# A fused kernel's first stage: one-row indices, counts by column, and a new order of loads and DVE work

## The reference

```python
# x (128, 64, 512), conditions (128,), weights (200, 64, 64), W1 (2048, 512), W2 (512, 2048)
w = weights[conditions]
c = jnp.einsum('bct,bcd->bdt', x, w)           # rows of 512

def ternarize(W, threshold=0.05):
    absW = jnp.abs(W)
    delta = threshold * jnp.max(absW)
    mask = absW > delta
    n = jnp.maximum(jnp.sum(mask), 1)
    alpha = jnp.sum(jnp.where(mask, absW, 0.0)) / n
    return alpha * jnp.sign(W) * mask

h = gelu(c @ ternarize(W1).T + b1)             # exact gelu
y = h @ ternarize(W2).T + b2
scale = jnp.max(jnp.abs(y)) / 7 + 1e-8
out = x + jnp.clip(jnp.round(y / scale), -7, 7) * scale
```

## Time and profile before

| | us |
|---|---|
| median of 3 runs (1003.8 to 1004.51) | 1003.95 |
| the profiled execution, its own time | 1004.09 |
| its span in the profile | 1002.2 |
| PE busy | 925.8 (92%) |
| DVE busy | 644.5 (64%) |
| ACT busy | 547.3 (55%) |
| POOL busy | 144.8 (14%) |

### The profile page before, as it was taken

The page is one execution under the profiler, slowest core; times in us unless marked ns, Lnnn a source line. Parts: engine busy times, 40 slices in busy tenths (PEclk is TensorE's granted clock), DMA queues, the critical chain, the costliest instruction groups (busy, mean ns, idle before and its releaser), DMA issues.

```text
span 1002.2 us, 14662 instructions
## 1 busy us (share of the span) xinstructions
PE 925.8 (92%) x5136; PEld 440.1 (44%) x5136; DVE 644.5 (64%) x1024; ACT 547.3 (55%) x690; POOL 144.8 (14%) x187
## 2 busy tenths in 40 slices
PE   2999999999999999999999999999999999999700
PEld 2544444444444444444444444444444444444300
DVE  7998576665656666656657666665666665633493
ACT  6886728274473827365372827446382836536190
POOL 4400030301203030200203030110303030000000
PEclk9999999999999999999999999999999999999955
DMA  9501103012212102111210301121210301204899
GB/s 341 154 2 43 43 14 82 10 42 44 50 42 51 43 10 59 32 45 42 52 42 25 69 10 42 46 48 42 52 42 10 69 23 44 84 0 168 313 385 390
DMA packets 24318, 77.86 MB, mean 78 GB/s; under 512 B 3952, under 2 KB 4080, under 8 KB 23792
## 3 DMA queue, kind: packets, MB, share of 16 engines
q1 hardware_dynamic: 20032, 73.41, 24.6%
q0 software_dynamic: 3840, 3.94, 1.4%
q10 hardware_dynamic: 432, 0.34, 0.1%
HBM read 60.89 MB, written 16.78 MB: 77 GB/s over the span
## 4 chain that ended last, share of the span: by engine, by line
PE 80%; issue 9%; DVE 5%; ACT 2%; DMA 1%; POOL 0%; SPq 0%; DVEq 0%; POOLq 0%; ACTq 0%
PE ps L433 39%; PE ps L443 37%; PE ps L413 3%; PE ps L494 3%; ACT y L706 1%; DMA y<-in_L_ffn_W 1%; DVE st L907 1%; DVE wts L866 1%; DVE wts L1046 1%; DVE wts L756 1%; DVE y L1046 0%; SPq L275 0%; DVE yc L772 0%; POOL odd L354 0%; DVE wts L911 0%
## 5 line engine op out<-in xcount | busy, mean ns | idle before, releaser
L433 PE MATMUL ps<-yc,wts 128*128 128x512 f16 x2048 | 444.9, 379 | 0.0
L443 PE MATMUL ps<-wts 128*128 128x512 f16 x1792 | 391.4, 379 | 0.0
L433 PEld LDWEIGHTS ps<-yc,wts 128*128 128x128 f16 x2048 | 200.4, 98 | 241.5 <-ACT g L610 0.4
L756 DVE SCALAR_TENSOR_TENSOR wts<-g,st,wts 128x512 f16<-128x512 f32 x256 | 186.4, 749 | 140.2 <-ACT wts L615 138.5
L610 ACT ACTIVATE g<-ps,b1t,st 128x512 f32<-128x512 f32 x256 | 197.9, 774 | 123.3 <-PE ps L433 106.7
L443 PEld LDWEIGHTS ps<-wts 128*128 128x128 f16 x1792 | 173.4, 98 | 204.8
L615 ACT ACTIVATE wts<-g,st 128x512 f16<-128x512 f32 x256 | 181.0, 713 | 0.0
L597 ACT ACTIVATE xs<-yx,st 128x2048 f16<-128x2048 f32 x28 | 56.1, 2002 | 136.8 <-DVE st L790 136.8
L365 POOL PARTITION_ALL_REDUCE st<-st x46 | 21.8, 473 | 663.3 <-DVE st L725 416.1
L348 POOL DMA_INDIRECT odd<-in_L_cond_weights,odd x112 | 110.1, 983 | 41.5 <-issue 30.0
L761 DVE SCALAR_TENSOR_TENSOR y<-ps,st,b2b 128x512 f32 (+1 forms) x56 | 41.6, 747 | 79.8 <-PE ps L443 79.7
(11 more groups left out here) (131 smaller groups left out, 366.8 us busy)
## 6 DMA issues: line engine op xcount, KB each, us to landing
yx<-in_x SPq DMA_DIRECT2D x56, 512.0 KB, 6.3
wts<-in_x SPq DMA_DIRECT2D x10, 512.0 KB, 5.4
out<-wts SPq DMA_DIRECT2D x10, 512.0 KB, 14.0
y<-in_L_ffn_W SPq DMA_DIRECT2D x8, 512.0 KB, 8.8
wts<-in_x SPq DMA_DIRECT2D x4, 1024.0 KB, 5.0
y<-in_L_ffn_W SPq DMA_DIRECT2D x4, 1024.0 KB, 20.5
y<-in_x SPq DMA_DIRECT2D x3, 1024.0 KB, 9.4
out<-wts SPq DMA_DIRECT2D x3, 1024.0 KB, 13.0
```

The costliest lines, as they stand in the source:

```text
L433: last = nc.tensor.matmul(psH[:, j % HB, :], T1T[:, j // HC, k, j % HC * P:(j % HC + 1) * P], csp[:, a, k, :], start=(k == 0 and a == 0), ...
L443: last = nc.tensor.matmul(psY[:, r % 2, :], hsp[:, a, j, r * P:(r + 1) * P], T2T[:, j, :], start=(j == 0 and a == 0), stop=(j == HT - 1 an ...
L756: nc.vector.scalar_tensor_tensor(out=hsp[:, 1, j, :], in0=g[:, j % HB, :], scalar=s_h, in1=hsp[:, 0, j, :], op0=ALU.mult, op1=ALU.subtract ...
```

## The change

Nothing in the loop is altered. In the first stage:

- **Indices.** The condition numbers are loaded once, into one row (`cond_row`, 512 bytes), and are turned into numbers there. One fp32 matmul of a row of ones against that row spreads them over 128 partitions in PSUM (`psIds`), and DVE makes the indices from that. The load of b1 is issued behind the first absolute value.
- **Loads.** x of block 0 is loaded ahead of the last two pieces of W1, not behind them.
- **ACT.** The maximum of x stands behind the sixth absolute value, `spread_w(0)` between the seventh and the eighth. `relu1(2)` stands before `spread_w(1)`, and ACT makes the sign of the third quarter of W1 (`sign1(2)`) before the gelus. The copies of c of block 1 stand beside tiles 8 and 11, before beside 3 and 5.
- **DVE.** The maximum of the gathered weights stands ahead of the wait for W1's maximum. The bound's chain and the first ternary column tile follow the first mask; masks 2 and 3 stand behind `low_c0`. `ternary1(2)` becomes a product of sign and mask (`signed1`) behind the scale of h, and `ternary1(3)` moves behind the second maximum of W2. The first quarter of `ternary2` is made in two halves; `t2_begun` marks the first.
- **Counts.** `count1` uses the mask as the stationary operand against one column of twos (64 matmuls with one column), so a partition holds one sum; the counts stand ahead of `first(0, 3)`. The count goes with the sum over |W| into one all-reduce of POOL.
- **PE.** After the index matmul come 120 matmuls of 128x128 fp16 whose results nobody reads. c of block 1 is made behind `first(0, 3)`, before behind `first(0, 0)`.

```diff
-        condb, idx, ids = odd_i[:, 0:B], odd_i[:, B:2 * B], odd_i[:, 2 * B:2 * B + BB]
+        cond_row, idx, ids = odd_i[0:1, 0:B], odd_i[:, B:2 * B], odd_i[:, 2 * B:2 * B + BB]
...
-            load_weight(w1s, W1.rearrange("p c k h -> p (c k h)"), LOADS, w1_loaded)
+            w1_v = W1.rearrange("p c k h -> p (c k h)")
+            load_weight(w1s, w1_v, LOADS, w1_loaded, range(LOADS - 2))
             load_direct(0)
+            load_weight(w1s, w1_v, LOADS, w1_loaded, range(LOADS - 2, LOADS))
             load_direct(1)
...
             all_max(max1_part, 1, m1r, m1, max1_all)
-            gather_direct(1, range(2, RT))
             pool.wait_ge(x0_summed, 1)
             all_max(xwb_part, 1, xwbr, xwb, xwb_all)
+            gather_direct(1, range(2, RT))
...
-                for n in range(WCH):
-                    last = nc.tensor.matmul(psN1, twos[:, :], quarter(mask1, c, n), start=(c == 0 and n == 0),
-                                            stop=(c == WCH - 1 and n == WCH - 1))
+                for n in range(QUARTER // P):
+                    last = nc.tensor.matmul(psN1, mask1[:, c * QUARTER + n * P:c * QUARTER + (n + 1) * P], twos[:, 0:1],
+                                            start=(c == 0 and n == 0), stop=(c == WCH - 1 and n == QUARTER // P - 1))
...
+            pe.wait_ge(id_row_made, 1)
+            nc.tensor.matmul(psIds, ones_f[0:1, :], id_row, start=True, stop=True).then_inc(ids_spread, 1)
+
             pe.wait_ge(consts_made, 1)
+            for _ in range(120):
+                nc.tensor.matmul(psH[:, 1, 0:P], twos[:, :], twos[:, :], start=True, stop=True)
             pe.wait_ge(xdirect_loaded[0], 16)
             pe.wait_ge(w_spread, 1)
             condition_direct(0, 0, psC)
             condition_direct(0, 1, psC0)
-            for c in range(WCH):
-                count1(c)
-
...
                 if j == HB - 1:
+                    for c in range(WCH):
+                        count1(c)
                     pe.wait_ge(n_read, 1)
                 first(0, j, wait_bank=j >= HB, wait_c=False)
-                if j == 0:
+                if j == HB - 1:
                     pe.wait_ge(xdirect_loaded[1], 16)
...
-            pe.wait_ge(t2_made, 1)
+            pe.wait_ge(t2_begun, 1)
...
-            act.dma_start(condb[:, :], cond.rearrange("(a b) -> a b", a=1).to_broadcast([P, B])).then_inc(cond_loaded, 16)
-            act.dma_start(b1t[:, :], b1).then_inc(b1_loaded, 16)
+            act.dma_start(cond_row, cond.rearrange("(a b) -> a b", a=1)).then_inc(cond_loaded, 16)
...
+            def sign1(c):
+                part = slice(c * QUARTER, (c + 1) * QUARTER)
+                nc.scalar.activation(t1_flat[:, part], w1s[:, part], ACT.Sign).then_inc(sign1_made, 1)
...
+            def signed1(c):
+
+                dve.wait_ge(sign1_made, c - 1)
+                dve.wait_ge(mask1_made, c + 1)
+                nc.vector.tensor_tensor(quarter(t1_flat, c), quarter(t1_flat, c), quarter(mask1, c), ALU.mult).then_inc(t1_made, 1)
...
-            ternary2(0)
+            ternary2(0, slice(0, 2), t2_begun, WCH)
+            ternary2(0, slice(2, HC))
```

95 lines of the change are left out of this document (55 added, 40 removed).

## The result

The changed kernel takes 1007.97 us (median of 6 runs, 1007.21 to 1008.35) against 1003.78 for the kernel before (6 runs, 1003.54 to 1004.51): a ratio of 1.0042, 95% interval 1.0031 to 1.0052. It is 4.2 us slower. The prediction said 1005.3 with a range up to 1007.2, and gave "slower by over 0.2%" a chance of 0.28. In the profiled execution (1007.80, span 1006.0 against 1002.2) the difference is 3.7 to 3.8 us, and the profile tells where each part of it comes from.

The account below looks back on a forecast made before the run. PE was taken as the bound (busy 92%), so only the end of its last gap counts: loads +1.8 and DVE's list -0.5 make it 1.3 us later. 1003.95 + 1.3, rounded up, gave 1005.3 us, range 1003.0 to 1007.2.

Parts of the forecast that it names:

- The chain through DVE: DVE's work from W1's threshold to PE's last awaited gelu: ended last by 0.2 us, would end 1.3 us later.
- the term for reading the count: On DVE: reading the count waits for PE's three tiles of 1.73 us and 64 one-column matmuls, +0.5 us.
- rival 1: PE's clock falls back in idle gaps before c of block 0 or the first tile: +2.2 to +3.0, 1006.5, chance 0.20.
- It decides from about 4 us of idle time on: Condition for rival 1: PE's idle gaps of 1 to 7 and 4 us bring the clock down from about 4 us.
- the second gap: PE idle after c of block 0 until 27.15: if the clock falls, the count is read up to 1.7 us later.
- The first gap's price: PE idle before c of block 0: if the clock falls, the second low_c0 waits for ACT, all behind 0.9 us later.
- the sign of rival 1: On PE in the changed profile: c of block 0 taking over 5 us would show rival 1.
- Taking the counts from the place where they held PE: On PE's chain: moving the counts behind the first tiles gives 2.2 - 1.9 = 0.3 us.
- The start of the chain: W1's threshold on DVE: x ahead +2.8, earlier loads -1.1, competing gathers and b1 +0.1; sum +1.8 us.
- Ternary W2 in halves: On DVE: the first quarter in two halves has twice the start of two instructions, +0.15 us.
- The first low part: On DVE: low_h(0) follows the scale of h by 2.1 us, not 2.3: -0.2 us.
- the worst of the clock: The worst of rival 1, left out of the range 1003.0 to 1007.2.

Follow-up runs that it names:

- x_between: row_only with x of block 0 loaded ahead of the last two pieces of W1, and ACT's order to it; 1004.55 us, ratio 1.0009.
- no_warmup: The changed kernel without the 120 idle matmuls at the start; 1006.82 us, ratio 1.0020.
- keep_clock: The changed kernel with 70 filler matmuls on PE between c of block 0 and the first tile; 1004.94 us, ratio 1.0013.
- row_only: The kernel before with the condition numbers in one row, spread by one matmul, and b1 loaded behind the first absolute value; 1003.30 us, ratio 0.9989.
- row_short_list: row_only with one-column counts, an earlier maximum of gathered weights, ternary W1's quarter 2 behind h's scale and quarter 3 as sign times mask; 1002.96 us, ratio 0.9992.
- Narrow_count: row_only with the counts by one-column matmuls at their old place, one column copied by DVE; 1003.62 us, ratio 0.9998.
- wide_short: row_short_list with the counts of the kernel before (16 matmuls of 512 columns, one reduction on DVE); 1001.55 us, ratio 0.9978.
- two_signs: keep_clock with one more sign on ACT and the fourth quarter of ternary W1 made as sign times mask on DVE; 1005.75 us, ratio 1.0018.
- quarter_back: keep_clock with ternary W1's quarter 2 ahead of the count's read, quarter 3 behind the scale of h, no sign on ACT; 1006.22 us, ratio 1.0023.

## Why the prediction was wrong

**What held.** PE never stops behind its last gap, and that gap's shift is the change of the span (3.69 against 3.8). The chain through DVE was the one that ended last. The first tile started at 27.45 (27.15). The product of sign and mask took 1.21 us and lay in the wait for the first high part. That x ahead of W1 costs more than the earlier start of the loads gives back held as well (x_between, 0.9 us above the kernel before).

**The step that failed** is the term for reading the count, +0.5. It was reckoned with "three tiles of 1.73 us", that is with the clock up, and the fall of the clock stood beside it as rival 1 with a chance of 0.20. The clock fell in both gaps of the profile, three tiles took 6.92 us and not 5.2, and DVE waited 2.25 us for the count.

What was off in rival 1 was "It decides from about 4 us of idle time on": the gaps were 3.3 and 4.7 us long, and in no_warmup the clock was down after 2.6 us of idle time behind c of block 0. What the earlier trace rows had shown was a fall seen some 5 us behind the last matmul of a long busy stretch; it was one case, and said only that the fall had come by then. The price of the second gap was right, "up to 1.7 later", where the wait grew by 1.75. The first gap's price, 0.9, wasn't paid: c of block 0 took 5.15 us, which the prediction had named as the sign of rival 1, but ACT had not to wait for its second half. In no_warmup, where c took 6.53, DVE waited 0.86 for it.

The keep_clock run shows this cause: with the fillers DVE's wait is 0.68, and the intervals of the two ratios don't meet. Its whole gain of 2.9 us can't be put down to the clock; in the profiles 1.6 of 2.7 can.

**A thing not seen at all** is what the old counts did. "Taking the counts from the place where they held PE" was priced at 0.3 us on PE's chain. They held PE, but at the upper level: behind them, 1.3 us of idle time (row_only) and 2.1 (x_between) left the clock at 1.00; with 64 one-column matmuls in their place it fell within 0.6 us of their end (row_short_list). Narrow_count and the pair row_short_list and wide_short price the edit alone at 0.9 and 1.4 us.

**Terms of the sum.** The start of the chain came 2.01 us later where 1.8 had been reckoned, in part by luck. The single edits give other terms: the small loads out of the way bring W1's last piece 1.65 us forward (row_only; 1.0 was taken), x in front of it takes it 2.3 back (x_between; 2.8 was taken), and together that is +0.7. The other 1.3 us is that the last piece landed late in this profile, 2.8 us behind the seventh, and no term stood for that. Ternary W2 in halves: 0.15 was taken, from no row, and 0.4 measured in the profile (3.60 to 4.00). The first low part was to follow the scale of h 0.2 us sooner; it followed after 2.25 (38.90 to 41.15), before after 2.27. The wait for the count: +0.5 taken, 2.25 measured. Those four make +0.2, +0.25, +0.2 and +1.75 of the 2.4 us by which the gap's shift (3.69) exceeds 1.3.

**The range** ended at 1007.2 and, in the prediction's words, left out "the worst of the clock": it has room for one gap's price (+3.0, 1006.9), with every other term at its middle. The start, the halves and the low part were above their middle (0.65 together), which makes 1007.6; the rest of 1007.97 is no more than executions of the changed kernel differ among themselves (1007.21 to 1008.35).

**Still open.** The last piece of W1 with x in between starts its maximum at 16.9 to 17.3 us in five profiles of this load order and at 18.2 to 18.4 in three (the changed kernel, two_signs, quarter_back). Why is not known, nor how often each happens; the order of landing isn't that of the queue alone. Which executions of keep_clock lost what is open too: the three slowest (1006.42 to 1007.39) have a mean granted clock of 0.972, the others 0.972 to 0.974, and that doesn't tell them apart.

## What to carry to other kernels

Before taking work from an engine whose speed depends on being busy, or moving it, look at what stands around it: the replaced matmuls were the reason why the next ones ran at full speed. Warming up costs and must reach to the work it is for; fixed fillers hold up what follows when they start late. And when a chain begins with the last byte of a load, nothing that can wait goes ahead of that byte: here one 1 MB block in front cost 2 us of a 1004 us kernel.
